# Three PSUM banks for a batch's scores and a fifth work bank in the dense attentions of a fused transformer trunk

## The reference

```
qh = (q @ Wq + bq).reshape(B, LQ, 16, 8)       kh, vh likewise from the context
scores = einsum('bhqd,bhkd->bhqk', qh, kh) / sqrt(8)
attn = softmax(scores, axis=-1)
out = einsum('bhqk,bhkd->bhqd', attn, vh).reshape(B, LQ, 128) @ Wo + bo
```

## Time and profile before

| | us |
|---|---|
| three runs | 1204.36, 1203.63, 1208.85 |
| median of them | 1204.36 |
| the profiled execution, its own time | 1201.54 |
| span of its trace | 1199.7 |

### The profile page before, as it was taken

One profiled execution on the slowest core, in us unless ns is written; L12 is line 12 of the kernel. 1 busy time (PEld: TensorE's weight loads), 2 busy tenths in 40 slices (PEclk: granted clock), 3 DMA queues, 4 the chain that ended last, 5 costly groups with the idle time before them and its releaser, 6 DMA issues.

```text
span 1199.7 us, 35823 instructions
## 1 busy us (share of the span) xinstructions
PE 907.3 (76%) x14340; PEld 679.3 (57%) x14340; DVE 826.9 (69%) x2234; ACT 708.5 (59%) x1441; POOL 556.3 (46%) x583
## 2 busy tenths in 40 slices
PE   2787758879999664688988589988298855788773
PEld 1455557736777444256665256766187733556663
DVE  4676647768878797688867577767465748766653
ACT  5777545666564665675566576576265574774331
POOL 3474744446557345254452322221552375657333
PEclk9788769989999977799999699999599867886787
DMA  4331132131010000100001000000213121111122
GB/s 109 94 90 36 52 101 79 51 82 37 29 31 26 31 22 25 47 21 12 4 4 45 1 3 4 4 3 2 84 56 105 52 71 44 37 36 32 58 85 84
DMA packets 63040, 53.75 MB, mean 45 GB/s; under 512 B 13915, under 2 KB 51291, under 8 KB 62685
## 3 DMA queue, kind: packets, MB, share of 16 engines
q1 hardware_dynamic: 57100, 42.25, 12.4%
q0 software_dynamic: 4096, 8.40, 2.3%
q10 hardware_dynamic: 1683, 0.81, 0.2%
HBM read 34.22 MB, written 16.25 MB: 42 GB/s over the span
## 4 chain that ended last, share of the span: by engine, by line
PE 32%; issue 26%; DVE 23%; ACT 10%; POOL 4%; DMA 2%; POOLq 1%; another core or an unknown queue 0%; ACTq 0%; SPq 0%; DVEq 0%
PE psum L742 9%; PE psum L1324 6%; PE psum L1342 3%; DVE area L2039 3%; DVE stats L2020 2%; PE psum L884 2%; PE psum L1344 1%; DVE x L2582 1%; PE psum L966 1%; DVE area L2212 1%; DVE area L2363 1%; DVE negm L2180 1%; POOL sorted_in L2995 1%; PE psum L749 1%; ACT area L1415 1%
## 5 line engine op out<-in xcount | busy, mean ns | idle before, releaser
L1415 ACT ACTIVATE area<-psum 128x512 bf16<-128x512 f32 (+2 forms) x164 | 85.6, 537 | 125.9 <-PE psum L742 67.3
L2039 DVE TENSOR_TENSOR area<-psum,area 128x512 bf16<-128x512 f32 (+3 forms) x156 | 92.8, 619 | 41.8 <-ACT area L1415 38.1
L2693 DVE TENSOR_TENSOR area<-area 128x512 bf16<-128x512 f32 x106 | 72.5, 689 | 63.1 <-ACT area L1935 41.7
L1324 PE MATMUL psum<-xT_hi,moe 128*128 128x128 bf16 x848 | 102.7, 233 | 6.0 <-issue 4.0
L2793 POOL TENSOR_TENSOR moe<-stage,moe 128x512 bf16<-128x512 f32 x47 | 54.4, 1159 | 112.1 <-ACT moe L1410 112.1
L1599 ACT ACTIVATE area<-psum 77x1024 f32<-77x1024 f32 (+1 forms) x96 | 92.7, 1017 | 18.8 <-PE psum L895 11.5
L1342 PE MATMUL psum<-moe,area 128*128 x424 | 88.9, 288 | 2.6 <-issue 1.2
L1324 PE MATMUL psum<-xT_lo,moe 128*128 128x128 bf16 x424 | 87.5, 233 | 1.2 <-issue 1.2
L1324 PEld LDWEIGHTS psum<-xT_hi,moe 128*128 x848 | 78.3, 105 | 10.9 <-issue 8.0
L1344 PE MATMUL psum<-moe,area 128*128 x424 | 81.7, 228 | 1.6 <-issue 1.6
L2786 POOL TENSOR_SCALAR rstd<-moments 128x4 f32<-128x4 f32 (+1 forms) x49 | 13.5, 275 | 145.9 <-DVE moments L2024 141.8
(11 more groups left out here) (278 smaller groups left out, 3082.6 us busy)
## 6 DMA issues: line engine op xcount, KB each, us to landing
area<-sorted_in SPq DMA_DIRECT2D x22, 256.0 KB, 4.0
sorted_out<-area SPq DMA_DIRECT2D x22, 256.0 KB
stage<-in_w_L0m SPq DMA_DIRECT2D x16, 256.0 KB
stage<-in_w_L2m SPq DMA_DIRECT2D x16, 256.0 KB
stage<-in_w_L3m SPq DMA_DIRECT2D x16, 256.0 KB
sorted_in<-area SPq DMA_DIRECT2D x2, 1472.0 KB, 7.3
stage<-in_w_L2a SPq DMA_DIRECT2D x8, 320.0 KB
stage<-in_w_L1x SPq DMA_DIRECT2D x6, 320.0 KB
```

Of the source, the lines that this page charges most:

```text
L1324: ins = pe.matmul(bank[:, S * c:S * c + S], lhsT, v, start=n == 0, stop=n == 2)
L1415: ins = act.activation(out, bank, ACT.Copy)
L2039: ins = dve.tensor_tensor(out, bank, high, ALU.subtract)
L2693: dve.tensor_tensor(R.HL[u], R.HF[u], upper(R.HF[u]), ALU.subtract).then_inc(K.tile_split, tiles.one())
```

## The change

- The scores of a batch lie in three banks. Half 0 keeps bank 0 and the first 128 columns of bank 1. Half 1's four matmuls of 128 keys write bank 2, and its two of 64 keys the last 128 columns of bank 1, so that its 640 columns are again one run, with the last tile in front (`tile_at` finds the tiles for `outputs`).
- `key_scores(b)` issues both halves' first matmuls and half 0's last ones, behind one wait for both exponentials of the batch before. Half 1's two last matmuls (`late_key_scores`) come behind the first row maximum of the step, and wait until the exponential of half 0 of the same batch is done. The other row maximum of the pair comes behind them.
- Bank 3 joins the work ring for the length of a dense stage: five banks, used in turn. The ring goes back to four at the stage's end. The index of a bank and its count of uses are kept for each use in place of t % 4 and t // 4.
- All matmuls, exponentials and reads are as many and as large as before.

In all other places of the diff `K.turn[key] % 4` becomes `K.turn[key]`.

```
@@ module, Trunk @@
+WORK_BANKS = (4, 5, 6, 7, 3)
...
         self.ST = self.psum[:, 0:4, :]
-        self.work = [self.psum[:, 4 + i, :] for i in range(4)]
+        self.work = [self.psum[:, i, :] for i in WORK_BANKS]
...
-        self.emptied = [sem(f"emptied{i}") for i in range(4)]
+        self.emptied = [sem(f"emptied{i}") for i in range(len(WORK_BANKS))]
...
     def emptied_at(self, key):
 
-        t = self.turn[key]
-        return self.emptied[t % 4], t // 4 + 1
+        return self.emptied[self.turn[key]], self.uses[key]
@@ Dense @@
+    LAST_AT = (0, BANK - S)
+    SCORES_AT = (0, 2 * BANK - S)
...
+    def tile_at(self, half, tile):
+
+        return S * ((tile + half) % 5)
@@ tensor_program @@
+    ring, used = collections.deque(range(4)), [0] * len(WORK_BANKS)
...
+    def work_banks(n):
+
+        while len(ring) > n:
+            ring.remove(len(ring) - 1)
+        while len(ring) < n:
+            ring.appendleft(len(ring))
+
     def take(*key):
 
-        t = turns.n
-        turns.one()
-        K.turn[key] = t
-        sem.wait_ge(K.emptied[t % 4], t // 4)
-        return K.work[t % 4]
+        i = ring.popleft()
+        ring.append(i)
+        sem.wait_ge(K.emptied[i], used[i])
+        used[i] += 1
+        K.turn[key], K.uses[key] = i, used[i]
+        return K.work[i]
 
@@ tensor_program, dense @@
         begin()
+        work_banks(5)
...
+        def first_scores(b, half):
+            j, u = b % GB, b // GB % 2
+            for i in range(4):
+                t, at = 2 * half + i // 2, 128 * (i % 2)
+                pe.matmul(K.ST[:, 2 * half, S * i:S * i + S], A.KX[u][:, t, j, at:at + 128],
+                          A.QS[u][:, t, S * j:S * j + S], start=True, stop=True)
+
+        def last_scores(b, half):
+            j, u = b % GB, b // GB % 2
+            for i in range(2):
+                t, at = 2 * half + i, A.LAST_AT[half]
+                ins = pe.matmul(K.ST[64 * i:64 * i + 64, 1, at:at + S], A.KX[u][:, t, j, 256:4 * CP],
+                                A.QS[u][:, t, S * j:S * j + S], start=True, stop=True)
+            ins.then_inc(K.scored, scored.one())
+
         def key_scores(b):
-            g, j, u = b // GB, b % GB, b // GB % 2
+            u = b // GB % 2
             sem.wait_ge(*K.emptied_at((name, "negm", b)))
             sem.wait_ge(K.head_rows_set, 4 * (A.order + 1))
             if u == 1:
                 sem.wait_ge(K.head_rows_copied, 16 * (A.order + 1))
-            for half in range(2):
-                if b >= 1:
-                    sem.wait_ge(K.exp_done, A.half0 + 2 * (b - 1) + half + 1)
-                for i in range(4):
-                    t, at = 2 * half + i // 2, 128 * (i % 2)
-                    pe.matmul(K.ST[:, 2 * half, S * i:S * i + S], A.KX[u][:, t, j, at:at + 128],
-                              A.QS[u][:, t, S * j:S * j + S], start=True, stop=True)
-                for i in range(2):
-                    t = 2 * half + i
-                    ins = pe.matmul(K.ST[64 * i:64 * i + 64, 2 * half + 1, 0:S], A.KX[u][:, t, j, 256:4 * CP],
-                                    A.QS[u][:, t, S * j:S * j + S], start=True, stop=True)
-                ins.then_inc(K.scored, scored.one())
+            if b >= 1:
+                sem.wait_ge(K.exp_done, A.half0 + 2 * b)
+            first_scores(b, 0)
+            last_scores(b, 0)
+            first_scores(b, 1)
+
+        def late_key_scores(b):
+            sem.wait_ge(K.exp_done, A.half0 + 2 * b + 1)
+            last_scores(b, 1)
 
@@ outputs(b): the same change for PL @@
-                    p = A.PH[n % 4][:, S * tile:S * tile + S]
+                    at = A.tile_at(half, tile)
+                    p = A.PH[n % 4][:, at:at + S]
@@ the loop over batches @@
             if 0 <= b - 2 < B:
                 key_scores(b - 2)
             if b < B:
-                row_maxima(b, (0, 1))
+                row_maxima(b, (0,))
+            if 0 <= b - 2 < B:
+                late_key_scores(b - 2)
+            if b < B:
+                row_maxima(b, (1,))
             if ahead < NG and b % GB == 3:
                 queries_rows(ahead, (0, 1))
...
+        work_banks(4)
         end()
@@ scalar_program, dense, exponentials @@
-            act.activation(A.PF[n % 4], K.psum[:, 2 * half:2 * half + 2, :].rearrange("p k n -> p (k n)")[:, 0:5 * S],
-                           ACT.Exp, scale=A.scale).then_inc(K.exp_done, exps.one())
+            at = A.SCORES_AT[half]
+            act.activation(A.PF[n % 4], K.psum[:, 0:3, :].rearrange("p k n -> p (k n)")[:, at:at + 5 * S], ACT.Exp,
+                           scale=A.scale).then_inc(K.exp_done, exps.one())
```

More of the change, by code:

```diff
@@ L2 @@
 import concourse.mybir as mybir
+import collections
 from contextlib import ExitStack
@@ L717, in tensor_program @@
     sem = Waiter(pe)
-    turns, fills, scored, hidden_n, contracted = Tally(), Tally(), Tally(), Tally(), Tally()
+    fills, scored, hidden_n, contracted = Tally(), Tally(), Tally(), Tally()
+    ring, used = collections.deque(range(4)), [0] * len(WORK_BANKS)
     xn, stages = Tally(), Tally()
@@ L1427, in bank_of @@
     def bank_of(key):
-        return K.work[K.turn[key] % 4]
+        return K.work[K.turn[key]]
     def normed(name, src, g, turn="x", behind=None):
@@ L1469, in layer_tokens @@
         act.activation(K.xT[:, xs], bank, ACT.Identity, bias=N.gain[1],
-                       scale=N.gain[0]).then_inc(K.emptied[K.turn[key] % 4], 1)
+                       scale=N.gain[0]).then_inc(K.emptied[K.turn[key]], 1)
         sem.wait_ge(*K.emptied_at(key))
@@ L1489, in tokens_turned @@
             sem.wait_ge(K.filled, K.fill[R.last_logits(g - 2)])
-        act.activation(K.xT[:, g % 2], bank_of(key), ACT.Copy).then_inc(K.emptied[K.turn[key] % 4], 1)
+        act.activation(K.xT[:, g % 2], bank_of(key), ACT.Copy).then_inc(K.emptied[K.turn[key]], 1)
     def gates():
@@ L1504, in router_hidden @@
         act.activation(R.RT[g % 2], bank_of(key), ACT.Silu,
-                       bias=K.col(R.router_hidden[1])).then_inc(K.emptied[K.turn[key] % 4], 1)
+                       bias=K.col(R.router_hidden[1])).then_inc(K.emptied[K.turn[key]], 1)
     def start():
@@ L1543, in token_tile @@
             ins = act.activation(K.xT[:, xs], bank, ACT.Identity, bias=gain[1], scale=gain[0])
-            ins.then_inc(K.emptied[K.turn[key] % 4], 1)
+            ins.then_inc(K.emptied[K.turn[key]], 1)
             sem.wait_ge(*K.emptied_at(key))
@@ L1587, in values @@
                 act.activation(A.Vs[s][0:A.L, a // hd:(a + n) // hd, :], v,
-                               ACT.Copy).then_inc(K.emptied[K.turn[key] % 4], 1)
+                               ACT.Copy).then_inc(K.emptied[K.turn[key]], 1)
         def exponentials(b, half):
@@ L1614, in turned @@
                 sem.wait_ge(*K.emptied_at((name, "scale", b - 2)))
-            act.activation(A.ON[b % 2], bank_of(key), ACT.Copy).then_inc(K.emptied[K.turn[key] % 4], 1)
+            act.activation(A.ON[b % 2], bank_of(key), ACT.Copy).then_inc(K.emptied[K.turn[key]], 1)
         def turn_outputs(b):
@@ L1830, in rounded_hidden @@
             act.activation(N.PW[n % 4][0], bank_of(key), ACT.Identity,
-                           bias=K.col("round8")).then_inc(K.emptied[K.turn[key] % 4], 1)
+                           bias=K.col("round8")).then_inc(K.emptied[K.turn[key]], 1)
         def rounded_result(g):
@@ L1867, in hidden @@
                 act.activation(N.HF[g % 2][:, c, :], bank_of(key), N.act_fn,
-                               bias=K.col(N.b1, c)).then_inc(K.emptied[K.turn[key] % 4], 1)
+                               bias=K.col(N.b1, c)).then_inc(K.emptied[K.turn[key]], 1)
         if N.pwl:
```

5 lines of the change are left out of this document (3 added, 2 removed).

## The result

The changed kernel takes 1227.5 us at the median of four runs (1220.9 to 1230.0), the kernel before, beside it, 1206.5 (four runs). The ratio is 1.018, with an interval of 1.015 to 1.022: slower by 1.8%, where 0.8% was forecast, and above the range. The profiled execution took 1220.93 us for a span of 1219.2, 19.4 us more than before's. The lines of the file that are shown have moved by 13 to 40 (L1095 is L1115 now, L1104 is L1124, L1121 is L1137, L1139 and L1142 are L1172 and L1176, L1765 is L1805, L2363 is L2403, L2372 is L2412).

A forecast was written before the change was run, and what follows sets the result against it. Hand-overs between engines, none over 76% busy, were taken to bound the kernel. L0x 6.6 - 0.6 = 6.0 plus L3x 6.1 - 0.6 - 1.7 = 3.8 gave 9.8 us on 1204.4: 1214; own range 1208 to 1222, eight in ten 1197 to 1225.

The forecast's parts named there:

- the replay: Dense-stage steps re-timed with the earlier trace's durations, counting delay at the next step's start: 6.6 us L0x, 6.1 L3x.
- step 5: L0x with ACT late: exponentials begin at 65.09, PE goes on at 65.84, and the step ends 1.4 us later.
- step 10: L0x with ACT prompt: the whole 2.00 us wait before L1104 goes, yet nothing is won; PE waits at maximum 2.
- the sum: Replayed losses per dense stage in steps without late ACT: 1.6 us (6, 7), 1.0 (10, 11), 0.4 (2, 3).
- steps 6 and 7: Dense stages: later `outputs`, queries' rows and reciprocal, less freed bank waits, make the two steps together 1.6 us longer.
- steps 10 and 11: Dense stages: the two steps together lose 1.0 us in each stage.
- the replay of the late steps, 5, 9, 13 and 17: Dense-stage steps with ACT late: PE held until half 0's exponential ends, delaying `outputs`; 1.4, 1.1, 0.7, 0.4 us in L0x.
- rival 3: Dense stages: more idle PE holds the granted clock down, adding 10 us to the forecast: 1224; chance 0.08.
- half of 45 us: Range's upper end: at most all ACT lateness plus 8 us of new waits makes 45; half was taken.
- The bank gains: Fifth bank in the dense stages: 0.6 us a stage plus 1.7 in L3x, 2.9 us faster if alone.
- L3x's step 3: `outputs(0)`, 3.48 us behind DVE's L2582 for a bank, gets another with five banks and runs beside it: 1.7 us gained.
- rival 1: Dense stages: fifth-bank gains of 17.4 us beat the new wait's 32 x 0.3: -8 us, 1196; chance 0.19.

The follow-up runs named there:

- the repeats: Changed kernel with half 1's four first matmuls issued 7, 12, 7 and 5 more times ahead of the late wait at steps 5, 9, 13, 17: 1191.5 us, ratio 1.007.
- the version without the wait: Changed kernel with both halves' last pairs issued before half 0 is reported to ACT, five banks, no wait between halves: 1194.0 us, ratio 0.991; again 1174.0, 0.993.
- the execution on the third chip: The changed kernel itself, nothing altered, timed again on another chip: 1204.6 us, ratio 1.017 of before.

## Why the prediction was wrong in size and right in direction

The two steps of L0x that the replay had taken as its patterns, in the timeline of the changed kernel: step 5, which answers to the earlier trace rows, and step 10, which answers to the earlier trace rows.

```profile
63.36 0.68 ACT L1805 ACTIVATE area<-psum 128x640 f32<-128x640 f32 x1
...
64.09 0.32 PE L1137 MATMUL psum<-area 128*64 128x128 bf16 x2 [3.74 <-ACT area L1805]
...
64.60 0.79 PE L1172 MATMUL psum<-area 128*128 128x72 bf16 x10
...
64.83 0.49 DVE L2403 TENSOR_REDUCE area<-psum 128x4 bf16<-128x320 f32 x1 [2.98 <-PE psum L1116]
...
65.50 0.80 PE L1172 MATMUL psum<-area 128*128 128x72 bf16 x10
...
67.30 2.12 PE L761 MATMUL psum<-area,bands 128*96 128x320 bf16 x8
...
103.71 0.25 PE L1137 MATMUL psum<-area 128*64 128x128 bf16 x2 [0.33 <-ACT area L1805]
...
105.16 0.22 PE L1124 MATMUL psum<-ident_bf,area 128*128 128x128 bf16 x1
...
107.20 0.28 PE L1115 MATMUL psum<-area 96*128 96x256 bf16 x1 [1.83 <-DVE area L2403]
```

In step 5 PE stands idle for 3.74 us and DVE for 2.98, until maximum 1 comes. Then PE goes on at the lower level: both groups of ten matmuls (0.79, 0.80 us) and the eight of L761 (2.12 us). Before, the first ten took 0.79 too, but at 63.59, beside ACT's lateness; the second ten took 0.52, and the eight 1.29. In step 10 ACT is prompt, and the matmuls keep the upper level.

**Where it was right.** The new wait decides, it stands where it was put, and most of what it costs is paid in the dense stages. The late pair has 48.3 us of idle PE ahead of it, all ended by ACT (at least 10 foretold). In step 10 the wait at L1104 (L1124 now) went and little was won: PE waits 1.83 us at maximum 2 instead, and the step is shorter by 0.55 us of the 2.00. In the prompt step the pair waits 0.33 us (0.25 foretold). ACT's gap between the halves is 0.41 us (0.4), its idle time 25.1 (22). DVE's idle time ahead of the reciprocal grew from 22.0 to 32.0 us. For the steps without a late ACT the sum came near: the wait in them costs 4 to 6 us by the runs (0.3 to 0.5%), 6 us by the sum (1.6 + 1.0 + 0.4 in each of two stages). That is partly luck. In the profiled pair steps 6 and 7 together are longer by 1.0 and 1.2 us for 1.6, and steps 10 and 11 by 0.2 and 2.6 for 1.0.

**The step that failed** is the replay of the late steps, 5, 9, 13 and 17: 1.4 + 1.1 + 0.7 + 0.4 for L0x and 0.8 + 1.2 + 0.7 + 0.4 for L3x, 6.7 us in all. The wait put into these steps alone costs 1.3 to 1.5%, 15 to 17 us. In the profiled pair step 5 of L0x became 3.2 us longer and not 1.4, step 13 2.5 and not 0.7; in L3x steps 5, 9 and 13 by 2.2, 3.3 and 2.8 against 0.8, 1.2 and 0.7. Steps 17 to 19 became 2.6 and 2.5 us longer against 0.4: the late pair of step 17 waits 2.52 and 2.73 us, and the stage's end moved by as much. Only L0x's step 9, 1.45 for 1.1, came out near its replay. Two things were left out of the replays:

- Their durations were those of the trace before, at the clock that PE had there. The replay let PE stand idle for 2 to 5 us and then go on at the same speed. It goes on at the lower level, and what follows is longer in that step. This is rival 3, with a chance of 0.08. Its price was near, 10 us on top of the forecast; what the repeats give back is 13.1 us, and a part of that the kernel before had lost too. The argument against it, that PE's activity falls only by a few per cent, did not hold it off: PE's busy share of the stretches went from 77 to 71% and from 72 to 68%, and the mean granted clock of the kernel fell with it from 0.863 to 0.849. The means of the stretches say little; the long falls of steps 5, 9 and 13 are seen behind PE's idle time in those steps. The Trainium skill (TensorE: Matmul & The Clock Gate, "What's actually happening") says that the slow clock is the default and activity lifts it, and the runs agree: the mean granted clock is 0.848 without the repeats and 0.879 with them. The forecast had the rule in hand and gave it too small a chance.
- The replay followed PE's queue to `outputs` and DVE's split, and took no account of DVE's reductions behind maximum 1. Maximum 1 is queued behind the wait as well, and DVE's 27.4 us of idle time ahead of the reductions, 4.6 before, were not in the forecast; of DVE's waits it named that of the reciprocal only. This part remains when PE is kept busy: 26.2 us there. How the rest of the loss is shared between this hand-over and the late `outputs` was not measured.

The premise that a microsecond lost in a dense stage is one of the kernel's held only roughly: of the 8.0 us by which L0x ended later, 2.3 were left in the expert layer behind it. The stages themselves are 8.2 and 10.5 us longer, where 6 and 4 were foretold. And the range's upper end was half of 45 us on 1204.4, which is 1227 and not 1225; the result, 1227.5, lies above both.

**The bank gains were too small as well**, which hid a part of the error: 2.9 us forecast, 9.0 measured beside the layout that has no wait, and 0.5% (about 5 us, with intervals that overlap) beside the layout with it. L3x's step 3, whose 1.7 us was more than half of the forecast gain, did not go as replayed: `outputs` did not run beside L2582's 5.08 us, for with five banks these adds take 2.29. Steps 2 and 3 together are 3.6 us shorter in the changed kernel than before all the same. So something was won there, in another way than the replay had it, and where the remaining gain comes in was not traced wait by wait. The 9.0 us lie between the forecast's 2.9 and rival 1's 17.4, and rival 1 was wrong on the wait.

**"It can't be had without."** The prediction read the rule on bank collisions (the Trainium skill, PSUM — Partial Sum Buffer, "PSUM bank collisions raise a hardware error") as: three banks for two halves are paid with a wait between them. The rule asks that no engine touch a bank and quadrant while another does; it does not ask for the order chosen here. With both halves' last columns written before half 0 is reported, the writer is done with the shared bank before the reader starts, and the kernel is 0.7 to 0.9% faster than before, and 2.5% faster than the changed one on the chip that ran both (1174.0 against 1204.6 us).

**The account**, in shares of before, starts from the version without the wait, -0.7 to -0.9%, of which the fifth bank makes 0.8. The wait in the late steps adds 1.3 to 1.5%, the wait in the others 0.3 to 0.5%. The remainder to the changed kernel's ratio is 0.7 to 0.8%; it holds the two kinds of wait coming together and ACT's gap between the halves, and was not measured by itself. The sum is +1.7 to +1.8%. Up to 1.0% of before in it are the clock's, by the repeats. Not tried: a kernel in which ACT is never late, by moving the normalization (L1520) in ACT's order, and the repeats in a kernel without the wait. What share of the clock's part belongs to step 11 of L3x, and what to the late steps themselves, stays open too.

## What to carry to other kernels

Before a wait is put into an in-order queue, ask what stands behind it and which engine has nothing else to do, and ask how late the releasing engine comes in its worst steps: some 19 us of waits spread over the prompt steps cost 4 to 6 us here, some 24 us of them in the eight steps in which ACT is late 15 to 17. A replay of durations holds only as long as the clock does: where it leaves PE idle for some microseconds, reckon what follows with its duration at the lower level too. And where two engines must not share a bank, look first for an issuing order in which the writer has finished with it before the reader is released.

## What the hardware showed that was not expected

- More work made the kernel faster. 31 repeats of four matmuls a stage, most of them in time that PE stood idle, took 1204.6 us to 1191.5 and the granted clock from 0.848 to 0.879.
- The clock does not answer alike to like waits. In one execution of the changed kernel step 11 ran at 1.00 in L0x (7.90 us) and at 0.61 in L3x (9.59 us), behind waits of 5.10 and 5.50 us in step 9 and of 1.83 and 1.74 us in step 10; in the execution on the third chip it ran at 0.61 and 9.63 us in L0x too. So this part of a kernel's time comes and goes between executions.
- One add of DVE took 5.56 us and its seven neighbours 0.34, beside four operations of GpSimd. With four banks it was so in all three traces, with five in none of ten, and another operation of DVE took 3.07 us in the changed kernel.
- The three chips differ by up to 1.8% on the kernel before (1205.0, 1186.6 and 1183.5 us), while the changed kernel's ratio is the same in both of its measurements, 1.018 and 1.017.
